# A four-layer network in one program: weights of the cross attentions read one stage ahead, its first pairs spread, and the routing of the last experts worked out by fewer operations

## The reference, cut to what matters

```python
def _L3_xattn_ref(query, key, value, mask, key_padding_mask, Wq, bq, Wk, bk, Wv, bv, Wo, bo):
    ...
    q, k, v = (split_heads(q), split_heads(k), split_heads(v))      # 16 heads of 16
    energy = jnp.einsum('bhqd,bhkd->bhqk', q, k) * scale
    energy = jnp.where(mask == 0, neg_inf, energy)
    ...
    attention = jax.nn.softmax(energy, axis=-1)
    out = jnp.einsum('bhqk,bhkd->bhqd', attention, v)
    return out @ Wo.T + bo

def _L3_ffn_ref(x, Wr, br, Wi, bi, Wg, bg, Wo, bo, gamma, beta):    # E, K = 8, 2
    probs = jax.nn.softmax(xf @ Wr + br, axis=-1)
    topw, topi = jax.lax.top_k(probs, K)
    topw = topw / jnp.sum(topw, axis=-1, keepdims=True)
    c = jnp.zeros((T, E), x.dtype).at[jnp.arange(T)[:, None], topi].set(topw)
    y = jax.vmap(_expert_ffn, ...)(xf, Wi, bi, Wg, bg, Wo, bo, gamma, beta)
    out = jnp.einsum('te,eth->th', c, y)
...
x = x + jnp.tanh(g_xattn[0]) * _L0_xattn_ref(_layernorm(x, axis=-1), ctx_1024, ctx_1024, ...)
x = x + jnp.tanh(g_ffn[0]) * _L0_ffn_ref(_layernorm(x, axis=-1), ...)
```

## Time and profile before

| | |
|---|---|
| Median of three runs | 2940.99 us |
| The profiled execution's own time | 2937.35 us |
| Its span | 2935.6 us |
| Mean granted clock of PE | 0.919 |
| PE, DVE, ACT, POOL busy | 88%, 61%, 46%, 38% |

### The profile page before, as it was taken

How to read it: one execution, slowest core, us unless ns; L and a number is a source line. 1 busy time by engine, 2 the same in 40 slices (tenths; PEclk the granted TensorE clock), 3 DMA queues, 4 the chain that set the end, 5 groups by cost and what they waited for, 6 DMA issues and landing times. The chain is left out here.

```text
span 2935.6 us, 57244 instructions
## 1 busy us (share of the span) xinstructions
PE 2572.4 (88%) x21432; PEld 2096.7 (71%) x21432; DVE 1801.1 (61%) x3917; ACT 1346.3 (46%) x2698; POOL 1127.6 (38%) x1409
## 2 busy tenths in 40 slices
PE   7999799997997999869699898888868994999995
PEld 7999487883876777636377666666746873999995
DVE  5666587125874343368488437787758874566765
ACT  4454366323663111247466433344433661555663
POOL 3444311003113333247612233554362113677773
PEclk9999699996998999979799999889977995999998
DMA  8888855327550000062466300000027733455663
GB/s 230 243 246 242 235 160 153 119 88 188 164 174 15 1 0 1 31 165 65 121 185 167 119 1 1 1 1 1 1 69 201 181 95 128 189 203 202 214 221 110
DMA packets 153628, 361.72 MB, mean 123 GB/s; under 512 B 26496, under 2 KB 110336, under 8 KB 138160
## 3 DMA queue, kind: packets, MB, share of 16 engines
q1 hardware_dynamic: 141632, 273.03, 33.0%
q0 software_dynamic: 11760, 85.51, 8.2%
HBM read 269.33 MB, written 88.67 MB: 122 GB/s over the span
## 5 line engine op out<-in xcount | busy, mean ns | idle before, releaser
L1235 ACT ACTIVATE arena<-ps 125x448 f32<-125x448 f32 x768 | 404.7, 545 | 325.9 <-PE ps L1129 321.9
L1269 DVE TENSOR_REDUCE arena<-ps 112x2 f32<-112x750 f32 x384 | 348.4, 931 | 82.2 <-PE ps L1113 79.3
L502 POOL TENSOR_SCALAR ln_var<-ln_mv 112x1 f32<-112x1 f32 x160 | 43.0, 269 | 768.1 <-DVE ln_mv L496 763.8
L3039 PE MATMUL ps<-moe_x_r,moe_w_r 128*128 128x256 f32 x2016 | 254.8, 288 | 9.2 <-DVE arena L3199 7.8
L1129 PEld LDWEIGHTS ps<-arena,wreg 98*125 98x125 bf16 x2304 | 215.8, 143 | 60.6 <-issue 18.9
L3039 PEld LDWEIGHTS ps<-moe_x_r,moe_w_r 128*128 128x128 f32 x2016 | 249.1, 195 | 12.0 <-DVE arena L3199 8.8
L1113 PE MATMUL ps<-wreg,arena 96*112 96x375 bf16 x768 | 217.7, 372 | 31.9 <-DMA arena<-query_parts 18.6
L1129 PE MATMUL ps<-arena,wreg 98*125 98x112 bf16 x2304 | 237.3, 228 | 3.7 <-ACT arena L1235 2.9
L1139 PE MATMUL ps<-arena 125*17 125x112 f32 x6144 | 199.2, 263 | 0.6 <-ACT arena L1235 0.6
L428 POOL TENSOR_TENSOR arena<-arena 128x375 bf16<-128x375 f32 x128 | 114.6, 918 | 166.4 <-ACT arena L365 166.4
L285 PE MATMUL ps<-kv_ctx_r,kv_w_r 128*128 128x376 f32 x768 | 145.7, 339 | 21.5 <-DVE kv_w_r L391 14.6
(11 more groups left out here) (363 smaller groups left out, 5879.4 us busy)
## 6 DMA issues: line engine op xcount, KB each, us to landing
wreg<-key_parts SPq DMA_DIRECT2D x288, 187.5 KB, 4.0
key_parts<-arena SPq DMA_DIRECT2D x128, 281.2 KB, 4.0
arena<-query_parts SPq DMA_DIRECT2D x108, 224.0 KB, 4.6
values<-arena SPq DMA_DIRECT2D x64, 357.0 KB
arena<-values SPq DMA_DIRECT2D x64, 357.0 KB
arena<-key_parts SPq DMA_DIRECT2D x96, 187.5 KB, 4.0
query_parts<-arena SPq DMA_DIRECT2D x40, 336.0 KB, 5.7
wreg<-in_e_w SPq DMA_DIRECT2D x16, 704.0 KB, 5.3
```

The source lines that it names most:

```text
L1235: act.activation(probs[k % PROBS], ps[0:KN, 4 + k % 2, 0:GT], ACT.Exp, scale=scale).then_inc(at_probs, 1)
L1269: dve.tensor_reduce(negmax[r % 2][:, 2 * p:2 * p + 2], ps[0:T, 2 * (p % 2):2 * (p % 2) + 2, 0:S2], AX.X, ALU.max, negate=True).then_inc(at ...
L3039: mm = pe.matmul(ps[:, f % 4, q * BS:(q + 1) * BS], w_r[wp][:, q, c, f * 128:(f + 1) * 128], x_r[u][xp][:, c, :], start=(n == 0 and c == 0 ...
```

## The change

1. **Weights ahead.** `QueryWeights` reads one transfer for each kind of weight and only the rows that are needed, and those of cross 2, 3 and 4 are read in the stage before (position experts, self, product key), those of cross 1 before the last stores of the context. Cross 4 reads its output weights and the router late in its own front.
2. **Queries.** The parts are laid out by part, then tile; the columns of the query weights are permuted (`by_halves`) so that a part of both tiles is one row-contiguous piece. One transfer stores a kind of a group. Group 0 is not stored: `spread_first` moves it from SBUF to SBUF in six transfers.
3. **Front and steps.** PE projects three groups; the fourth's four pieces stand between pairs of batch 0 (`LAST_GROUP_AT`). Only pairs 0 and 1 of batch 1 are made before step 0; the rest, and those of batches 2 and 3, stand in steps 0 and 1 by the table `FIRST_PAIRS` (12 and 10 pairs). The maxima rows have a semaphore of their own (`row_in`). SP's order is new. POOL fills the rows of ones between low parts.
4. **Logits.** `LOGITS_LATE` is 5, not 3; the logits in the tail are spread; cross 4 makes 11 of the 16 for the routed stage (`RoutedRouter`).
5. **Routing.** The counts are summed in PSUM by 15 more matmuls (bf16 one-hots); the blocks ahead come from one product and one reduction; both choices are found by one reduction; the block number comes from adding and subtracting 1.5 x 2^23; `in_block` has two rows, one of them made by ACT.
6. **Query and self stage.** Two rows and four weight transfers; group 0 is spread directly.
7. POOL's deviations are placed differently.

The diff, cut to its core:

```diff
             def load(self, sp):
-                sp.dma_start(self.w[:, self.needed], a["attn_w"][self.s, :, self.needed]).then_inc(loaded, 16)
-                for r in range(2):
+                for k in self.now:
+                    sp.dma_start(self.w[k], a["attn_w"][self.s, :, k]).then_inc(loaded, 16)
+                for r in self.rows:
                     sp.dma_start(attn_rows[:, r, :], a["attn_rows"][self.s, r].partition_broadcast(128)).then_inc(loaded, 16)
...
+            def spread_first(self, sp, kind, dest, order, arrived):
+
+                for level, made in enumerate((part_hi, part_mid, part_lo)):
+                    sp.wait_ge(made, self.q0 + (kind + 1) * DC)
+                    for j, q in enumerate(order):
+                        if q == level:
+                            sp.dma_start(dest[spread(j), :, :].rearrange("d h n -> d (h n)"),
+                                         self.parts[0][:, q, kind * DC:(kind + 1) * DC, :].rearrange("p t n -> p (t n)")).then_inc(arrived, 16)
...
-        PAIR_AT = {0: 0, 1: 1, 3: 2, 4: 3, 6: 4, 7: 5, 9: 6, 10: 7}
+        PAIR_AT = {0: (0,), 1: (1,), 3: (2,), 4: (3,), 6: (4,), 7: (5,), 9: (6,), 10: (7,)}
+        LAST_GROUP_AT = {1: (0, 0), 3: (0, 1), 5: (1, 0), 7: (1, 1)}
+        FIRST_PAIRS = ({0: ((1, 2), (1, 3)), 1: ((1, 4),), 2: ((1, 5),), 3: ((1, 6),), 4: ((1, 7),), 6: ((2, 0),), 7: ((2, 1),),
...
+        MAXIMA_AT = (6, 3)
...
-        LOGITS_AT, LOGITS_LATE = 2 * T + 32, 3
+        LOGITS_AT, LOGITS_LATE = 2 * T + 32, 5
...
                 load_keys(sp, keys[0], kv, 0, 0)
                 if masked:
-                    for b in range(RING - 1):
-                        load_masks(b, b)
-                else:
-                    load_keys(sp, keys[1], kv, 1, 1)
-                q.store(sp, 0)
-                q.stored(sp, 0)
-                load_queries(0, range(len(Q_PART)))
-                q.store(sp, 1)
-                load_keys(sp, keys[1 + (not masked)], kv, 1 + (not masked), 1 + (not masked))
-                for g in range(2, G):
+                    load_masks(0, 0)
+                q.spread_first(sp, 0, group_q[0], Q_PART, group_in[0])
+                if masked:
+                    load_masks(1, 1)
+                weights.load_late(sp)
+                load_keys(sp, keys[1], kv, 1, 1)
+                for g in range(1, G - 1):
                     q.store(sp, g)
                 load_values(0, 0)
                 if masked:
-                    load_keys(sp, keys[2], kv, 2, 2)
-                rows(0, 0)
-                for b in range(1, RING - 1):
-                    load_values(b, b)
+                    load_masks(2, 2)
+                rows(0)
+                load_keys(sp, keys[2], kv, 2, 2)
+                load_values(1, 1)
                 norm.load(sp)
-                q.stored(sp, G - 1)
-                load_queries(1, range(len(Q_PART)))
...
-                q.project(pe)
-                for b in range(2):
-                    arrived(b, b, turn0)
-                    for p in range(PAIRS):
-                        pair(b, b, p)
-                    if b == 0:
-                        maxima(0, 0)
+                pe.wait_ge(loaded, q.ready)
+                q.project(pe, range(G - 1))
+                arrived(0, 0, turn0)
+                for p in range(PAIRS):
+                    pair(0, 0, p)
+                    if p in LAST_GROUP_AT:
+                        tile, chunk = LAST_GROUP_AT[p]
+                        q.project_tile(pe, G - 1, tile, (chunk,))
+                arrived(1, 1, turn0)
+                pair(1, 1, 0)
+                maxima(0, 0)
+                pair(1, 1, 1)
...
-                pe.matmul(ps[0:T, 1, 0:B * E], before, both.rearrange("p b e -> p (b e)"), start=True, stop=True)
                 pe.matmul(ps[:, 2, 0:B * E], ones, both.rearrange("p b e -> p (b e)"), start=True, stop=True).then_inc(m_prefix, 1)
+                pe.matmul(ps[0:T, 1, 0:B * E], before, both.rearrange("p b e -> p (b e)"), start=True, stop=False)
+                for b in range(B - 1):
+                    mm = pe.matmul(ps[0:T, 1, (b + 1) * E:B * E].rearrange("p (b e) -> p b e", e=E), ones[:, 0:T],
+                                   both[:, b:b + 1, :].broadcast_to([T, B - 1 - b, E]), start=False, stop=(b == B - 2))
...
-                for b in range(B):
-                    link(dve.tensor_tensor(run[:, b + 1, :], run[:, b, :], counts[:, b, :], ALU.add))
...
+                link(dve.tensor_reduce(of_expert, ps[:, 2, 0:B * E].rearrange("p (b e) -> p e b", e=E), AX.X, ALU.add))
...
-                for e in range(1, E):
-                    link(dve.tensor_tensor(first[:, e:e + 1], first[:, e - 1:e], blocks_of[:, e - 1:e], ALU.add))
+                link(dve.tensor_tensor(blocks_ahead, ahead, blocks_of.unsqueeze(1).broadcast_to([128, E, E]), ALU.mult))
+                link(dve.tensor_reduce(first, blocks_ahead, AX.X, ALU.add))
```

444 lines of the change are left out of this document (268 added, 176 removed).

## The result

| | before | after |
|---|---|---|
| median of the runs, us | 2939.66 (2929.93 to 2943.34, 4 runs) | 2891.09 (2890.62 to 2895.43, 4 runs) |
| ratio, 95% interval | | 0.9846 (0.9823 to 0.987) |
| profiled execution, us | 2937.35 | 2895.43 |
| its span, us | 2935.6 | 2893.7 |

The change is 49 us faster where 66 were forecast. The direction and the range (2850 to 2906) hold, the size is three quarters.

The account below looks back on a forecast made before the run. PE, busy 88%, was taken to lose time waiting at stage starts. Cross starts 47.3 plus routed start 22.0 less costs 3 gave 66.3 us: 2937.35 becomes 2871.0, stated as 2875 for the median, range 2850 to 2906.

Parts of the forecast that it names:

- The cross starts: Starts of four cross stages: first exponential at +28.5 us after the barrier (cross 4 +30.5), gaining 59.2 together, net 47.3.
- clock rival: Pairs at cross starts: full clock throughout gives 2858 us, chance 0.18; half clock throughout gives 2902, chance 0.20.
- the moved pairs: Six of batch 1's pairs per cross stage, moved into steps 0 and 1; 5.6 us of DVE work a stage.
- Given back: Cross steps 0 and 1, longer by moved pairs: 3.8 us in cross 1 to 3, 0.5 in cross 4, together 11.9.
- the exponentials come but later steps 1 to 3 are long: Sign in the cross stages that would show the forecast wrong; no size given.
- slower rival: Cross stages: rows 0, 1 and 2 each land 10.7 us from issue to use, against 3.2 taken; 2965 us, chance 0.03.
- The routed start: Routed stage's start: logits 8.3, router 2.4, adds 3.7, placement 7.6; first expert matmul 22.0 us sooner, at +36.6.
- What costs: Losses: eleven logits in cross 4's tail 2 us, query stage's wait for rows 1; together 3.
- Tail of cross 4: Eleven batches' logits moved into the end of cross 4, mostly hidden in norm waits: cost 2 us (0 to 8.3).
- rival on the weights: Routed start: a later part of the weights' gather or split ends last, losing 7.6 and some 4 us; 2885, chance 0.10.

Follow-up runs that it names:

- few-keys run: Changed kernel with only one head's keys of batches 4 and 5 loaded in each cross stage; 2896.7 us beside 2954.0 of the kernel before.
- the last experiment: Changed kernel with POOL's gather of the first block's tokens ahead of its first weight split in the routed stage; 2895.3 us in one run.
- rows first: Changed kernel with maxima rows of batches 2 and 3 issued ahead of keys 4 and 5; 2910.3 us beside 2957.4 of the kernel before (0.9844).
- three edits: Changed kernel with rows 2 and 3 ahead of keys 4 and 5, last group's store at step 3, old POOL norm order; 2897.9 us (0.9817), 2886.0 (0.9864).

## Why the prediction was right or wrong

**The cross starts: right.** The sum of the four first exponentials was to fall by 59.2 us and fell by 58.0 (175.3 to 117.3). By stage it missed by -0.7, -2.4, +2.1 and +2.3 us, which nearly cancel. In cross 1 the terms are: PE at the barrier within 0.1 us; the first pair at +14.7, where +13 was taken; 8.8 us to the last reduction (8.7); 1.2 to the issue of the rows (1.5); the rows used 2.6 us after their issue began (3.2); 0.5 to ACT (1.1), and nothing of the 1 us for hand-overs. The clock in the pairs was 0.86, 1.00, 0.79 and 0.72 in the four stages, from one clock rival towards the other. At full clock the moved pairs were to be caught up; in cross 2, where the pairs had it, steps 0 to 2 took 14.2 us more than before, so that half of the rival does not hold.

**Given back: the step that failed.** The forecast charged 11.9 us ("I charge 3.8 in each of cross 1 to 3"), with 22.5 as the end, and 40.9 came. It counted reductions on DVE and left out that the first three steps end on transfers. The prediction named the sign of it itself ("the exponentials come but later steps 1 to 3 are long"), and the sign came, in steps 1 and 2. By the few-keys run 15.0 are pairs and hand-overs. Of the remaining 26, 11 go with 0.67 MB of a store that nobody wants before batch 12 if it alone is moved, 9 with the place of the rows of batches 2 and 3 if they alone are, 16 to 17 with both, and 24 to 26 if keys 4 and 5 are not loaded. By kind, some 17 us are waits of PE and 10 are its clock behind them (14.66 us for step 2 of cross 2, where before it took 10.59). The rows to see it in were shown: DMA share 0.89 from 333.4 to 349.4 and a row used 10.7 us after its issue. They were used for the slower rival only, as if rows either came at once or in 10.7 us. Those of batch 0 came at once; those of batch 2 came after 6.9 us from the start of their issue, because a start that is 13 us earlier does not make the bytes come earlier: from the barrier to the end of step 1 cross 1 moved 14.0 MB at 220 GB/s before and 13.2 at 223 after. From barrier to step 3 the four stages took 319.0 us before and 302.0 after, and that is all that the starts kept: 17 us. The chain of waits had been shortened on one resource and now ended on another.

**The routed start: right in size.** 20.3 us to the first expert matmul (22.0 forecast), 23.5 over the stage. The gather was issued at +29.3, where +29.5 was forecast for its index; the missing 1.7 us lie behind it, 9.0 us from the gather to the first expert matmul, against 7.1 before (2489.54 to 2496.59). As in the cross stages it is a transfer behind others: the forecast weighed the split against the gather's issue, and neither ended last. DVE's small operations were slow beside POOL's split, 1.19 against 0.18 us, some 2.5 us over the chain; as the last experiment shows, a gather that is 2.5 us earlier gains nothing, so this costs nothing here. The Trainium skill, "SBUF — State Buffer", section "Who interferes with whom", has DVE and GpSimd share one port pair, and by that rule the forecast weighed 3 us; the trace agrees with the slowing and not with a price in time.

**What costs: right in size.** Tail of cross 4 1.9 (2 forecast). The query stage was forecast 1 us longer, for the four transfers ahead of the rows; its first matmul did come 1.2 us later in the stage, but the stage ended 3.1 us sooner. Its last store, one transfer where there were two, seems to land sooner, by ACT's idle time at the barrier, before and after:

```profile
1276.42 0.20 ACT L1476 ACTIVATE idle<-one 128x1 f32<-128x1 f32 x1 [7.01 <-SPq L192]
```

```profile
1263.62 0.20 ACT L1555 ACTIVATE idle<-one 128x1 f32<-128x1 f32 x1 [3.28 <-SPq L192]
```

The lora and self stages gained 3.7 and 2.1 us in the profiled pair; in other profiles of the change lora took 323 to 327 us and self 150 to 154, so no cause is claimed.

**The clock.** In cross 2 the pairs ran at a granted clock of 1.00 directly behind the projection, elsewhere at 0.72 to 0.86. Behind waits of 2.1 to 5.8 us step 2 ran at 0.68 to 0.87, and the forecast had no place for that price. The Trainium skill, "TensorE: Matmul & The Clock Gate", Part 1, has the array fall to 1.2 GHz behind idleness and return to 2.4 with sustained activity; the trace agrees in cross 2 and behind these waits. The runs also have a clock of 0.72 in a step with no wait over 1.11 us (rows first, cross 3) and one of 1.00 behind a wait of 2.24 us (three edits, cross 1), so a wait alone does not tell the clock.

**Two slips that changed nothing.** The rival on the weights adds up to 2886.6 (2875 + 7.6 + 4), not 2885. The rows of batch 0 were used 6.4 us after their issue in cross 1 (343.39 to the first scores at 349.75), not 7.1, which is the time to the exponential.

Sum of the misses: +29 given back, +1 at the starts, +4 context (1.4 by the weights, the rest open), +2 in cross 3's tail, -1.5 routed, -4 query and -6 lora and self: 66 becomes some 42 in the profiled pair, and 49 by the medians. The 10 us of the last two were not forecast, so that the size came out at three quarters is in part luck.

## What to carry to other kernels

When a stage's start is shortened, add up the bytes that must land before each of its next steps and divide by the rate that the trace shows at a full queue; the start can keep no more than that sum leaves. On a shared queue, put the small transfer that gates a step ahead of bulk, and put stores that are wanted late behind the crowded stretch, but not into the next one. Price each wait on PE twice: once for itself and once for the half clock that may follow it. Before moving a request ahead, ask whether its data stand behind others: the tokens were asked for 2.5 us sooner and came at the same time.
